# Step numbers, SyncE order and gather buffers of a fused attention and mixture-of-experts kernel

## The reference, cut to what matters

```python
x = L0_attn_x                       # 16 batches x 512 rows x 256
x = _layernorm(x + attention(x))    # 16 heads of 16, rotary, alibi, softmax, projection
# feed forward, on the normalised x
shared = silu(X @ sW1 + sb1) @ sW2 + sb2
logits = einsum("btd,ed->bte", X, routing_W) + expert_bias     # 8 experts
top_vals, top_idx = top_k(sqrt(softplus(logits)), 2)
routed = sum over the two chosen experts e of top_vals * (silu(X @ rW1[e] + rb1[e]) @ rW2[e] + rb2[e])
x = _layernorm(x + shared + routed)
```

## Time and profile before

| | us |
|---|---|
| runs of the kernel before | 1664.29, 1664.18, 1665.5 |
| median | 1664.29 |
| the profiled execution | 1663.59 |
| its span, first to last instruction | 1661.8 |
| PE busy | 1458.4 |
| DVE busy | 1171.7 |
| ACT busy | 1019.3 |
| POOL busy | 723.9 |

### The profile page before, as it was taken

How to read it: one execution, slowest core, us unless ns; L and a number is a source line. 1 busy time by engine, 2 the same in 40 slices (tenths; PEclk the granted TensorE clock), 3 DMA queues, 4 the chain that set the end, 5 groups by cost and what they waited for, 6 DMA issues and landing times.

```text
span 1661.8 us, 33130 instructions
## 1 busy us (share of the span) xinstructions
PE 1458.4 (88%) x11110; PEld 801.2 (48%) x11110; DVE 1171.7 (71%) x2631; ACT 1019.3 (61%) x1742; POOL 723.9 (44%) x655
## 2 busy tenths in 40 slices
PE   7987999999999889899999899988888999896467
PEld 4433444444444435555555544454455555564345
DVE  7665777878778787666666677857776577645674
ACT  1465666666767656666677576666566587675242
POOL 2233353635545343541535253533666344255630
PEclk8789899999999989999999999999999899998789
DMA  7334243434343324454545433443566566686531
GB/s 208 115 109 147 91 124 101 129 108 132 102 123 116 115 92 141 132 175 139 178 138 165 130 120 116 128 139 120 166 214 222 177 217 209 192 257 212 168 106 51
DMA packets 185349, 242.00 MB, mean 146 GB/s; under 512 B 67239, under 2 KB 104190, under 8 KB 185182
## 3 DMA queue, kind: packets, MB, share of 16 engines
q1 hardware_dynamic: 154746, 181.18, 36.4%
q0 software_dynamic: 10752, 29.37, 5.4%
q10 hardware_dynamic: 19684, 29.33, 5.0%
HBM read 152.53 MB, written 91.44 MB: 147 GB/s over the span
## 4 chain that ended last, share of the span: by engine, by line
PE 51%; DVE 15%; SPq 14%; DMA 10%; issue 6%; POOL 2%; ACT 2%; POOLq 0%; ACTq 0%; DVEq 0%
PE pS L641 15%; PE pV L683 9%; PE pG L707 6%; DVE negm L932 5%; PE pG L729 3%; PE pG L716 3%; SPq L390 2%; DMA xg<-d_x 2%; PE pS L647 2%; DMA d_rec<-scr 2%; PE pG L810 2%; SPq L459 2%; PE pG L818 2%; SPq L499 1%; DMA d_sum<-pvs 1%
## 5 line engine op out<-in xcount | busy, mean ns | idle before, releaser
L932 DVE TENSOR_REDUCE negm<-pS 128x1 f32<-128x512 f32 x1024 | 659.6, 683 | 336.4 <-PE pS L647 329.6
L1368 ACT ACTIVATE ee<-pT,slp 128x512 f32<-128x512 f32 x1024 | 649.0, 684 | 216.8 <-PE pT L668 215.2
L641 PE MATMUL pS<-ka,qa 62*128 62x512 f32 x1024 | 485.4, 509 | 81.0 <-DVE negm L932 68.3
L662 PE MATMUL pT<-qa,ka 64*128 64x512 f32 x1024 | 480.9, 504 | 0.2 <-ACT ee L1368 0.2
L641 PEld LDWEIGHTS pS<-ka,qa 62*128 62x128 f32 x1024 | 198.4, 194 | 330.0 <-issue 312.8
L683 PE MATMUL pV<-ee,vv 128*32 128x512 f32 (+1 forms) x2048 | 286.8, 633 | 0.0
L647 PE MATMUL pS<-mAB,tri 64*128 64x64 bf16 x2048 | 243.6, 200 | 0.0
L668 PE MATMUL pT<-mAB,tri 64*128 64x64 bf16 x2048 | 239.9, 198 | 0.0
L1555 POOL TENSOR_TENSOR raw<-raw,rope 128x512 f32<-128x512 f32 x61 | 78.2, 1282 | 330.0 <-DVE sh L966 329.9
L662 PEld LDWEIGHTS pT<-qa,ka 64*128 64x128 f32 x1024 | 195.6, 191 | 4.5 <-issue 3.1
L647 PEld LDWEIGHTS pS<-mAB,tri 64*128 64x128 bf16 x2048 | 119.8, 99 | 139.6 <-issue 107.3
(11 more groups left out here) (186 smaller groups left out, 2192.8 us busy)
## 6 DMA issues: line engine op xcount, KB each, us to landing
d_part<-parts SPq DMA_DIRECT2D x63, 512.0 KB, 2.8
qa<-d_part SPq DMA_DIRECT2D x378, 64.0 KB
wb<-in_wb SPq DMA_DIRECT2D x77, 256.5 KB
xg<-d_x SPq DMA_DIRECT2D x77, 256.0 KB, 2.9
d_y<-yb ACTq DMA_DIRECT2D x77, 256.0 KB, 2.6
ka<-d_part SPq DMA_DIRECT2D x128, 128.0 KB
xT<-in_xT SPq DMA_DIRECT2D x16, 512.0 KB
ka<-d_part SPq DMA_DIRECT2D x128, 64.0 KB
```

The costliest lines, as they stand in the source:

```text
L641: e.matmul(pS[:, k, :], qa[g % 4][r, i, t * 128:t * 128 + 128].bitcast(F32R), ka[g % 4][r, i, :].bitcast(F32R), start=True, stop=False)
L662: e.matmul(pT[:, k, :], ka[g % 4][r, i, kt * 128:kt * 128 + 128].bitcast(F32R), qa[g % 4][r, i, :].bitcast(F32R), start=True, stop=False)
L932: e.tensor_reduce(negm[:, g % 2, j, t + k:t + k + 1], pS[:, k, :], AX, ALU.max, negate=True).then_inc(s_max, 1)
L1368: e.activation(ee[:, k, d % 7, :], pT[:, k, :], ACT.Exp, scale=slp[:, 6, h:h + 1]).then_inc(s_exp, 1)
```

## The change

The diff gives new step numbers to many jobs. On SP the store of sums is due one step earlier, `assemble` two steps later, block loads one step earlier, `base_out` four later; the one-off loads and preparations (`LATE`, `PREP`, `PADS`) three later. On PE the two tiles of a V half, of a projection half, and the two downs get other steps. POOL's rotary steps, pair add and last scatter come one or two steps earlier. Blocks of group 0 from the 26th on come two steps later, the last four of group 1 two steps apart and no longer three.

The finals of batches 6 to 13 get step numbers of their own (`FINAL_STEPS`): gathers at 0, 0, 1, 1, adds at 6 to 9, `base_in` at 2. From the 24th gather on there are nine tiles in place of three (`gathered`, `ggl`): the three `gg`, the rotary tiles `raw` and `sh`, and the halves of `qa[0]` and `ka[0]`. A gather waits for the add nine before it. The experts of batch 14 begin at step 530 (541 before), ahead of the projection of batch 15 at 541 (538 before), those of batch 15 at 560 (566 before); the weights of batch 14's first four experts are loaded at 514 to 517 (536 to 539 before).

```diff
--- before.py
+++ after.py
@@ -30,19 +30,19 @@
 
 QK = ((-23, -22), (-18, -17), (-11, -7), (-5, -1))
 SHUFFLE = (2, 2, 2, 2)
-ROPE = (1, 1, 1, 3, 3)
+ROPE = (1, 1, 1, 2, 2)
 PARTS_OUT = 5
-V = ((10, 12), (15, 17))
+V = ((11, 12), (17, 19))
 XT_LOAD = -41
 X_LOAD = 43
 
-ASSEMBLE = -6
+ASSEMBLE = -4
 M_SPLIT, M_OUT, M_IN = (-1, -1, 2)
 EVAC = 24
-SUMS_OUT, SUMS_IN, RECIP, REC_OUT, REC_IN, SCALE = (2, 2, 5, 5, 6, 8)
-PAIR = 11
-BIASX = 55
-PROJ = ((58, 61), (65, 65))
+SUMS_OUT, SUMS_IN, RECIP, REC_OUT, REC_IN, SCALE = (1, 2, 5, 5, 6, 8)
+PAIR = 9
+BIASX = 56
+PROJ = ((61, 61), (62, 65))
 RESIDUAL = (61, 65)
 VAR1 = 66
 NORM1 = (68, 68)
@@ -53,33 +53,35 @@
 TOP2 = (74, 75)
 RANK = 77
 PLACE = 77
-SCATTER = (78, 79, 80, 81, 82, 83, 84, 85)
-UP = (77, 78)
-GATE = 83
-DOWN = (87, 89)
-BASE_OUT = 93
+SCATTER = (78, 79, 80, 81, 82, 83, 84, 84)
+UP = (76, 77)
+GATE = 85
+DOWN = (87, 87)
+BASE_OUT = 97
 
 EXPS = 76
 SOFTPLUS = (78, 99)
 POW = 104
 
-LAST_EXPS, LAST_SOFTPLUS, LAST_POW = (78, (80, 81), 85)
-
-LOADB, TURNB, UPB, GATEB, DOWNB, STOREB = (-2, 0, 1, 2, 3, 4)
+LAST_EXPS, LAST_SOFTPLUS, LAST_POW = (76, (77, 78), 79)
+
+LOADB, TURNB, UPB, GATEB, DOWNB, STOREB = (-3, 0, 1, 2, 3, 4)
 
 
 
 GROUPS = (6, 6, 2)
-BLOCKS_AT = ((90, 4.0, 25, 250, 4.0), (92, 2.0, 27, 146, 3.0), (92, 1.0, 11, 103, 2.0))
-FINALS_AT = ((278, 13), (158, 5), (125, 6))
+BLOCKS_AT = ((90, 4.0, 25, 252, 4.0), (92, 2.0, 27, 146, 2.0), (92, 1.0, 11, 103, 2.0))
+FINALS_AT = ((278, 13, 6, 356, 13), (158, 5, 6, 300, 5), (126, 5, 2, 156, 6))
 
 
 DENSE = 2
-DENSE_AT = ((93, 1), (86, 1))
-LOADD, GATED, DOWND = (-5, 1, 2)
-WEIGHTS, VAR3, NORM3, OUTD = (0, 24, 25, 27)
-BASE_IN, GATHER, ADD, VAR2, NORM2, OUT = (-1, (1, 2, 2, 4), (3, 4, 5, 6), 6, 8, 9)
-LATE, PREP, PADS = 11, (18, 20, 22, 24), 40
+DENSE_AT = ((82, 1), (80, 1))
+LOADD, GATED, DOWND = (-16, 1, 2)
+WEIGHTS, VAR3, NORM3, OUTD = (-1, 21, 23, 24)
+
+BASE_IN, GATHER, ADD, VAR2, NORM2, OUT = range(6)
+FINAL_STEPS = ((-1, (1, 2, 2, 4), (3, 4, 5, 6), 6, 8, 9), (2, (0, 0, 1, 1), (6, 7, 8, 9), 9, 10, 11))
+LATE, PREP, PADS = (14, (21, 23, 25, 27), 43)
 
 WARM = (5, 6, 4, 4, 5)
 NG = 3
@@ -98,8 +100,11 @@
 JMAX, TMAX = max(NBLOCKS), 2 * max(GROUPS)
 BLOCK_OF = {32 * LAST_OF[g] + (at + int(j * per) if j < n else at2 + int((j - n) * per2)): FIRST_BLOCK[g] + j
             for g, (at, per, n, at2, per2) in enumerate(BLOCKS_AT) for j in range(NBLOCKS[g])}
-FINAL_OF = {32 * LAST_OF[g] + at + int(k * per): LAST_OF[g] + 1 - GROUPS[g] + k
-            for g, (at, per) in enumerate(FINALS_AT) for k in range(GROUPS[g])}
+FINAL_OF = {32 * LAST_OF[g] + (at + int(k * per) if k < n else at2 + int((k - n) * per2)): LAST_OF[g] + 1 - GROUPS[g] + k
+            for g, (at, per, n, at2, per2) in enumerate(FINALS_AT) for k in range(GROUPS[g])}
+
+NGG, NGL = 3, 9
+FIRST_LATE = 4 * GROUPS[0]
 DENSE_OF = {32 * (SPARSE + k) + at + x * per: E * k + x for k, (at, per) in enumerate(DENSE_AT) for x in range(E)}
 
 
@@ -143,9 +148,22 @@
     return BLOCK_OF.get(s - at, -1)
 
 
-def final_due(s, at):
-
-    return FINAL_OF.get(s - at, -1)
+def final_due(s, step, t=0):
+
+    for kind, steps in enumerate(FINAL_STEPS):
+        at = steps[step][t] if step in (GATHER, ADD) else steps[step]
+        b = FINAL_OF.get(s - at, -1)
+        if b >= 0 and (b >= GROUPS[0]) == (kind == 1):
+            return b
+    return -1
+
+
+def gathered(k):
+
+    if k < FIRST_LATE:
+        return k % NGG, k // NGG + 1
+    i, n = (k - FIRST_LATE) % NGL, (k - FIRST_LATE) // NGL + 1
+    return i, n + (len(range(i, FIRST_LATE, NGG)) if i < NGG else 0)
 
 
 def dense_due(s, at):
@@ -278,7 +296,7 @@
 
     bd = sb("bd", [128, E])
     comb = sb("comb", [128, 2, DENSE, 4, E])
-    gg = [sb(f"gg{i}", [128, 2, C]) for i in range(3)]
+    gg = [sb(f"gg{i}", [128, 2, C]) for i in range(NGG)]
     bs = [sb(f"bs{i}", [128, 4, C]) for i in range(2)]
 
     pS = ps("pS", [128, 2, T])
@@ -304,6 +322,8 @@
     bias2 = [yb[0][0:E + 1, 0, :], yb[0][0:E + 1, 1, :], yb[1][0:E + 1, 0, :]]
 
     raw_q, sh_q = (gg[i][:, :, :].rearrange("p k c -> p (k c)") for i in range(2))
+    ggl = [x[:, :, :] for x in gg] + [x[:, :].rearrange("p (k c) -> p k c", k=2) for x in (raw, sh)]
+    ggl += [x[0][:, i, :].rearrange("p (k c) -> p k c", k=2) for x in (qa, ka) for i in range(2)]
     parts_q = bs[0][:, :, :].rearrange("p (k t) c -> p k (t c)", k=2)
     hot = ee[:, 1, 0, 0:H]
     bpos = ee[:, 0, 0:4, :].rearrange("p a t -> p (a t)")[:, 0:30 * 64].rearrange("p (r e) -> p r e", e=64)
@@ -327,7 +347,7 @@
     out_w = [sem(f"out_w{i}") for i in range(2)]
     y_w = [sem(f"y_w{i}") for i in range(3)]
     bs_in = [sem(f"bs_in{i}") for i in range(2)]
-    gg_in = [sem(f"gg_in{i}") for i in range(3)]
+    gg_in = [sem(f"gg_in{i}") for i in range(NGL)]
     xg_in = [sem(f"xg_in{i}") for i in range(NX)]
     wb_in = [sem(f"wb_in{i}") for i in range(4)]
     qk_in = [sem(f"qk_in{i}") for i in range(4)]
@@ -1188,10 +1208,11 @@
             if t == 0:
                 e.wait_ge(s_act, GROUP_OF[b] + 1)
                 e.wait_ge(bs_in[b % 2], 16 * (b // 2 + 1))
-            e.wait_ge(gg_in[k % 3], 32 * (k // 3 + 1))
-            link(e.scalar_tensor_tensor(x_, gg[k % 3][:, 0, :], wts[:, b, 0, t:t + 1], x_, ALU.mult, ALU.add))
-            linked()
-            e.scalar_tensor_tensor(x_, gg[k % 3][:, 1, :], wts[:, b, 1, t:t + 1], x_, ALU.mult, ALU.add).then_inc(s_add, 1)
+            i, n = gathered(k)
+            e.wait_ge(gg_in[i], 32 * n)
+            link(e.scalar_tensor_tensor(x_, ggl[i][:, 0, :], wts[:, b, 0, t:t + 1], x_, ALU.mult, ALU.add))
+            linked()
+            e.scalar_tensor_tensor(x_, ggl[i][:, 1, :], wts[:, b, 1, t:t + 1], x_, ALU.mult, ALU.add).then_inc(s_add, 1)
             e.wait_ge(s_add, k + 1)
             link(e.bn_stats(st[:, 1, t, :], x_))
 
@@ -1328,7 +1349,7 @@
             if (b := due(s, GATE)) >= 0:
                 gate(b)
             for t in range(4):
-                if (b := final_due(s, ADD[t])) >= 0:
+                if (b := final_due(s, ADD, t)) >= 0:
                     add_experts(b, t)
             if (b := final_due(s, VAR2)) >= 0:
                 variances(b, 1)
@@ -1596,11 +1617,21 @@
             for i in range(3):
                 e.wait_ge(y_w[i], 16 * ((FIRST_BLOCK[g + 1] + 2 - i) // 3))
             e.wait_ge(s_posy, g + 1)
-            if k > 2:
+            i, held = gathered(k)
+            if k >= FIRST_LATE + NGL:
+                e.wait_ge(s_add, k - NGL + 1)
+            elif k >= FIRST_LATE:
+                if k < FIRST_LATE + NGG:
+                    e.wait_ge(s_add, FIRST_LATE)
+                elif k < FIRST_LATE + NGG + 2:
+                    e.wait_ge(s_part, 4 * NB)
+                else:
+                    e.wait_ge(s_t, 16 * (4 * NB - 3))
+            elif k > 2:
                 e.wait_ge(s_add, k - 2)
             for n in range(2):
-                e.indirect_dma_start(gg[k % 3][:, n, :], None, d_y[g],
-                                     bass.IndirectOffsetOnAxis(posy[:, b, n, t:t + 1], 0)).then_inc(gg_in[k % 3], 16)
+                e.indirect_dma_start(ggl[i][:, n, :], None, d_y[g],
+                                     bass.IndirectOffsetOnAxis(posy[:, b, n, t:t + 1], 0)).then_inc(gg_in[i], 16)
 
         def add_pair(p):
 
@@ -1644,7 +1675,7 @@
                 e.tensor_tensor(wts[:, b0:b0 + ALL_GROUPS[g], :, :].rearrange("p b n t -> p (b n t)"), sp[:, 1, 0:N],
                                 halves[:, 0:1].broadcast_to([128, N]), ALU.pow).then_inc(s_act, 1)
             for t in range(4):
-                if (b := final_due(s, GATHER[t])) >= 0:
+                if (b := final_due(s, GATHER, t)) >= 0:
                     gather(b, t)
             for i in range(4):
                 for k in range(5):
```

## The result

The changed kernel took 1592.9 us (median of four runs, 1591.31 to 1594.63) against 1664.24 for the kernel before in the same set: a ratio of 0.9583, 95% interval 0.9547 to 0.962. That is 71 us less. I had forecast 36 less, 1628, with a range of 1608 to 1651: the direction was right, the size was half, and the time lies 15 us under the range.

What follows compares the result with a forecast made beforehand. PE's own work was taken to bound plain batches, with late block loads and the end's gap as stalls. Block loads -13.7 and -8.1, weights +3, end -17.1 sum to -35.9 from 1664.29: 1628 us, range 1608 to 1651.

Steps and rivals of the forecast that it cites:

- What bounds the kernel, and where the stalls are: Whole kernel: plain batches near PE's own work; 38.7 us of PE waits for block rows; PE mostly idle from 1520 to 1560.
- I take 0.8 of group 0's 17.1 us, and half of group 1's 16.2; group 2 gets nothing: Body, SyncE's new order of block loads: PE's waits for block rows fall, saving 13.7 us and 8.1 us.
- My upper bound of 33.3: Body, loads of blocks: the most that the new queue order could save, with bounds of 0 and 33.3 us.
- The work of both engines is unchanged and the row of waits small, so I take 0: Body, new steps for PE's jobs (V, projection, up, down): no gain or loss, 0 us.
- bounds -59 to +46: Body, PE jobs: up to 59 us gained if 4.2 us of waits fill, 46 lost if doubled steps starve DVE.
- My own sign of being wrong: Body: the forecast is wrong if, among other signs, plain batches leave 74 to 76 us.
- +3 for the weights: Body, batch 14's expert weights loaded earlier, in a stretch of busy DMA: costs 3 us, between 0 and 4.1.
- the 4 that stood beside it: Weights' load: by the Trainium skill's rule of shared DMA queues, the full 4.1 us falls on other loads.
- The end, -17.1: After attention: gathers run ahead and batch 14's experts precede batch 15's projection, saving 17.1 us, bounds 5 and 25.
- the rival of an end without gain: End: POOL's in-order rstd holds gathers and batch 14's experts hold the projection, so no gain; 1645.5 us, chance 0.18.
- The body without gain: Body: SP stays late, each wait that goes replaced by the next in its order; 1650 us, chance 0.15.
- The slower one: Body: doubled PE steps, three a batch at 1.1 us, starve DVE and ACT; 1675 us, chance 0.07.

Runs made afterwards that it cites:

- two pairs: Changed kernel with LOADD -16 to -5 (weights of batch 14's experts loaded later), beside the changed kernel: 1631.10 against 1634.54 us, and 1631.70 against 1631.46.
- Taking back the order: Changed kernel with batch 14's experts back behind batch 15's projection (DENSE_AT 82 to 93, LOADD -16 to -5): 1596.59 us, ratio 0.9606.
- taking back the ring: Changed kernel with three gather tiles in place of nine (NGL 3) and the old steps of the finals: 1599.83 us, ratio 0.9625.
- the first run: Kernel before with only SyncE's queue order changed (SUMS_OUT 2 to 1, ASSEMBLE -6 to -4, LOADB -2 to -3): 1620.34 us against 1661.56, ratio 0.9737.
- The two later sets: The changed kernel run again in the fifth and sixth sets: 1634.54 us against 1672.61 before, and 1631.46 against 1670.20.

## Why the prediction was wrong, by its steps

**What bounds the kernel, and where the stalls are: right.** Loads of blocks late behind `assemble` and the stop before the sums, the end's gap waiting for the pair add. SyncE's new order is as I drew it.

**"I take 0.8 of group 0's 17.1 us, and half of group 1's 16.2; group 2 gets nothing": the first failed step, a term mis-sized.** The queue's order was put at 21.8 us and gave 41.2 alone. As idle time the 21.8 came true: PE's idle time in attention fell by 21.1 us. The make-up was luck: the wait for xg went from 38.7 to 2.6 us and not to some 17, and other waits, above all those for row maxima, took back 15 of the 36, ka and m rows 4.1 of it (11.6 to 15.7). What failed is that I priced a stall at its row in the list of waits, with PE's work as a constant. It isn't: 18.2 of the 39.3 us in attention are the same matmuls in less time, at a higher mean clock. My upper bound of 33.3 for this term was thus no bound.

**"The work of both engines is unchanged and the row of waits small, so I take 0": the second failed step.** The places took a plain batch to 73.0 to 73.8 us, three quarters of it from V and the projection. I had the 4.2 us of stalls from the earlier trace rows and called their filling the upper bound of a zero; I didn't look where in the batch they lay. Single rows would have told: stalls of 0.48, 0.48 and 0.50 us in thin steps, and the new numbers put halves of jobs into them. Alone this is worth 8.0 us; with the queue in order, places and first steps together are worth 18.1 (1620.34 to 1602.19), of bounds -59 to +46. My own sign of being wrong, a plain batch outside 74 to 76, came up here.

**+3 for the weights.** Not shown: +3.4 and -0.2 in two pairs. They can't tell 3 from 0, nor from the 4 that stood beside it.

**The end, -17.1: right in mechanism, 3.8 too much.** Measured from the last exp, forecast and after:

| | forecast | after |
|---|---|---|
| first add of expert 0, batch 14 | 22.9 | 22.6 |
| add 7 begins | 52.0 | 55.2 |
| pair add | 46.5 | 45.9 |
| x1 of batch 15 ready | 68.3 | 73.8 |
| first add of its experts | 94.1 | 98.9 |
| last add | 121.7 | 125.5 |
| end | 133.2 | 137.0 |

(us after the last exp, which is 1511.5 before and 1453.7 after.) The projection came in one piece at 1507.81, as I had it. VectorE's first and last adds of batch 14's experts, and then PE's rows from the projection to the turn that waits for x1:

```profile
1476.25 1.66 DVE L1247 SCALAR_TENSOR_TENSOR x<-pS,comb,x 128x256 f32<-128x256 f32 x4 [2.28 <-PE pS L866]
1508.88 1.66 DVE L1247 SCALAR_TENSOR_TENSOR x<-pT,comb,x 128x256 f32<-128x256 f32 x4
```

```profile
1507.81 3.62 PE L749 MATMUL pG<-wp,pvs 128*128 128x256 f32 x16
1527.62 1.94 PE L761 MATMUL pG<-idf,x 128*128 128x128 f32 x8 [16.20 <-ACT x L1433]
```

Eight adds took 32.6 us where I had 29, since VectorE takes the finals' adds between them (3.2 late), and `norm1` came another 2.2 late, behind `rstd` and `norm2` of a final. The chain after x1 was 1.7 us quicker than I had it. Taking back the order costs 7 us and taking back the ring 7 to 10, so neither half came to nothing, and the rival of an end without gain fell.

**The rivals.** The body without gain fell at the first run. The slower one, doubled steps that starve VectorE, needed 0.85 us in three places. At most one place has a trace of it, the stall behind the downs, up by 0.2 to 0.5 us, and two downs in a step alone did not make that.

**The range.** It was closed at 1608 because I took the waits of a list as all that could be had. The full row of xg waits and the end alone give 1664.3 - 38.7 - 17.1 = 1608.5; with 1.2 us of filled stalls in each of 14 batches (17) the same views reach 1592. That this meets the time is luck: idle time fell by 21.1 us and not by 38.7, and the clock, which no row of waits holds, made up the rest. Still, the range should have held both rows. The two later sets, 1634.5 and 1631.5 us, lie within my range and near my 36 us of gain; that is luck as well, since the body's larger gain and the stops of some 25 us, which I had not thought of, cancel there.

## What to carry to other kernels

A stall of TensorE for a load costs more than its own length where the clock falls behind it: with the queue in order, 21.1 us of idle time went and 18.2 us of busy time with it. Compare PE's busy time over the same instructions, not only the list of waits, and look at the mean clock of all executions before trusting one: here the busy time of kernels with the same stalls strayed by 10 us. Before an edit of places is put at nothing, look up the stalls inside one repetition, row by row, and see whether the new places fall into them. A queue that is late for one consumer is late for all: here the wait ahead of a load of sums was worth more (30 us) than the ten loads that stood in front of the block (19). In the stretch of group 0, a gain elsewhere showed only once the queue was in time.

## What the runs showed that I had not expected

Sets on the same code differ by 40 us for the changed kernel and by 6 to 11 for the one before, with stops of TensorE, VectorE and ScalarE at fixed steps while the DMAs run at a high share. The kernel before took 1662.91 us in one set and 1672.61 in another on the same chip, so it is not a matter of the chip alone. A single set of runs, however tight (1591.31 to 1594.63), doesn't tell that there is such a condition.
